# Expert weights loaded in the attention tail, two down projections per row half, and a new order of shared and routed pairs in a mixture-of-experts decoder block

## The chip, the cores and the metric

The kernel runs on one core of one Trainium2 chip. Its time is the device time of one launch in microseconds (us). TensorE is written PE, VectorE DVE, ScalarE ACT, GpSimd POOL and SyncE SP, as in the profile; SP computes nothing and issues most of the DMAs.

## The reference

One decoder layer in fp32 on 4096 tokens (64 sequences of 64) of width 256. Two attention blocks come first, then a mixture of experts: each token has 8 of 64 small experts, and a shared one that all tokens use.

```
x = LN(x + self_attention(x));  x = LN(x + cross_attention(x, ctx))
topv, topi = top_k(x @ gate_w.T, 8);  rw = softmax(topv)
for a routed expert e of a token:  (silu(x @ gate_e.T) * (x @ up_e.T)) @ down_e.T * rw_e     # 64 inner columns
shared: sigmoid(x @ g1.T) * ((silu(x @ sh_gate.T) * (x @ sh_up.T)) @ sh_down.T)
x = LN(x + sum of the 8 routed + shared)
```

## The kernel before

Three phases follow each other, with a clearing of semaphores and a barrier of all engines between them.

**Attention phase.** 32 tiles of 128 tokens go through a software pipeline of six stages, a to f; a step of the pipeline works on six tiles at once, each in another stage. POOL scatters the finished rows of a tile, once per chosen expert, into `slot_scratch`, a DRAM table with a region per expert (`scatter`, L484, 8 indirect DMAs a tile). The rows also go to `token_row_scratch` and the routing data to `route_scratch`, by SP (L322, L328). At the end POOL waits until its scatters have landed.

**Expert phase.** A step works on a pair of row tiles, 2 x 128 rows. The 16 shared pairs (`SHARED_STEPS`) take rows of `token_row_scratch` in order, and only then come 160 sparse pairs (`SPARSE_STEPS`, 320 routed tiles) from `slot_scratch`. Which rows and which expert a routed tile has is found out on the chip: DVE makes tables (`table_counts` to `table_starts`, spread over steps 0 to 6), SP writes them to DRAM and reads them back (`pass_tables`) and takes each tile's address from them (`load_sparse`). For a step s the engines do:

- SP: load of the rows into `x_in[s % 8]`, 8 steps ahead (L1274 for shared pairs, two issues at L1298 for sparse ones)
- PE, in iteration i: `turn_x(i)` (4 transposes, L1377), `gate_and_up(i-1)` (4 matmuls, L1396), `turn_inner(i-2)` (2 transposes, L1405), `project(i-3)` (2 down projections of 64 rows by 256 columns, both on `dp[0:64]`, L1417)
- ACT: copies of the transposes and the silu
- DVE: gate times up, the copy of the result out of `bank_y` into `y[s % 4]` (`copy_y`, L1616, L1620), and three small operations for the destination rows
- POOL: two indirect DMAs of 128 rows per sparse pair to `expert_out_scratch` (`scatter`, L1347); a shared pair is stored by SP (L1260)

`copy_y(s)` waits until `y[s % 4]` has left. The weights of the experts (`gu` 8.4 MB, `dp` 4.2 MB) are loaded in this phase by SP, a group of three pairs of experts per shared step (`load_group`). From sparse pair 8 on, DVE also extracts the routing weights, one operation of 128 x 512 per step, 96 in all (`find_weights`).

**Combine phase.** 32 tiles: the 9 rows of a token are read back, weighted, summed and normalised.

## Time and profile before

| | |
|---|---|
| three timed runs | 1800.71, 1806.1 and 1807.99 us; median 1806.1 |
| profiled execution | 1804.36 us, its span 1802.4 us |
| attention phase, until POOL begins the expert phase | 0 to 1094.5 us |
| expert phase until POOL's first scatter | 1094.5 to 1200.5 us |
| expert phase, POOL's 320 scatters | 1200.5 to 1640.4 us |
| combine phase | 1651.3 us to the end |

A row of a timeline has the start, the duration, the engine, the line, the operation, what it writes and reads, and how many are merged; in brackets is the idle time of the engine before it and what ended it. "issue" is time in which nothing that the profile shows was waited for. PE matmuls are pipelined and their modelled ends overlap, so a stage's length is read from one start to the next. PE's records count two for an fp32 matmul and one for a transpose.

### The profile page before, as it was taken

To read this page: it belongs to the slowest core of one execution; us is meant where nothing else is said; L and a number is where in the kernel's file an instruction comes from. 1 tells how busy PE (TensorE), PEld (TensorE's weight loads), DVE (VectorE), ACT (ScalarE), POOL (GpSimd) and SP (SyncE) were. 2 spreads that over 40 slices of the span, in tenths; PEclk is the share of its full clock that TensorE was granted. 3 is DMA by queue.
4 is the path that set the end of the run, shared out by engine and by line. 5 is a ranking of instruction groups with operands and counts; after the bars stand their busy time and mean duration, and the time that the engine had idled before them with its cause. 6 is when DMAs were issued, how large, how long until landed. Compare 5 with 4: busy or idle time off the path is not lost. (4 is left out here: it accounts for less than half of the span.)

```text
span 1802.4 us, 34145 instructions
## 1 busy us (share of the span) xinstructions
PE 1475.3 (82%) x9600; PEld 1233.7 (68%) x9600; DVE 1319.6 (73%) x3879; ACT 694.7 (39%) x1462; POOL 1109.3 (62%) x1090
## 2 busy tenths in 40 slices
PE   3679999999999899999999855779999999992000
PEld 2568888888888787888888744567777777771000
DVE  3458888888888888888888843147777765553898
ACT  3235444545453444444443412124444444441221
POOL 3328676767676667677776641027777777774444
PEclk8789999999999999999999977579999999996555
DMA  5861212121212112121212117976655556642886
GB/s 197 287 201 50 84 49 77 54 79 51 76 56 74 56 63 69 53 79 47 85 47 71 45 70 230 256 214 191 188 187 185 184 182 189 190 120 99 294 298 241
DMA packets 161421, 237.36 MB, mean 132 GB/s; under 512 B 28044, under 2 KB 135578, under 8 KB 156836
## 3 DMA queue, kind: packets, MB, share of 16 engines
q1 hardware_dynamic: 127636, 160.73, 29.2%
q0 software_dynamic: 27648, 69.28, 10.4%
q10 hardware_dynamic: 6032, 6.13, 1.0%
q8 instruction: 45, 0.74, 0.2%
q14 instruction: 60, 0.49, 0.1%
HBM read 127.47 MB, written 116.93 MB: 136 GB/s over the span
## 5 line engine op out<-in xcount | busy, mean ns | idle before, releaser
L1347 POOL DMA_INDIRECT expert_out_scratch<-y,target x320 | 319.1, 997 | 225.5 <-issue 107.4
L484 POOL DMA_INDIRECT slot_scratch<-xrow x256 | 272.2, 1063 | 187.8 <-DVE xrow L1100 111.6
L1438 ACT ACTIVATE x_turned<-bank_x 128x512 f32<-128x512 f32 x176 | 105.1, 597 | 281.1 <-PE bank_x L1377 281.0
L523 PE MATMUL bank_c<-wq_w,x1t 128*128 128x512 f32 x768 | 193.2, 403 | 15.4 <-DVE q_work L942 11.7
L1417 PE MATMUL bank_y<-dp,inter_t 64*128 (+1 forms) x704 | 205.7, 414 | 0.0
L1396 PE MATMUL bank_g<-gu,x_turned 128*128 (+1 forms) x1408 | 195.6, 284 | 0.0
L669 PE MATMUL bank_d<-wo_w,o2t 128*128 128x256 f32 x1536 | 193.4, 286 | 2.0 <-DVE o2t L858 2.0
L669 PEld LDWEIGHTS bank_d<-wo_w,o2t 128*128 128x128 f32 x1536 | 187.6, 192 | 3.1 <-DVE o2t L858 2.7
L1616 DVE COPY y<-bank_y 128x512 f32<-128x512 f32 x160 | 110.6, 691 | 97.1 <-PE bank_y L1417 97.1
L429 POOL TENSOR_TENSOR q_rs<-q_ve,minus_half 128x8 f32<-128x8 f32 x64 | 137.4, 2147 | 71.3 <-DVE q_ve L933 67.6
L523 PEld LDWEIGHTS bank_c<-wq_w,x1t 128*128 128x128 f32 x768 | 142.3, 190 | 56.6 <-DVE q_work L942 21.0
L1396 PEld LDWEIGHTS bank_g<-gu,x_turned 128*128 128x128 f32 x1408 | 180.4, 200 | 0.7 <-issue 0.7
L1377 PE MATMUL bank_x<-identity,x_rows 128*128 128x128 f32 x704 | 120.8, 296 | 48.6 <-DMA x_rows<-token_row_scratch 39.5
L1417 PEld LDWEIGHTS bank_y<-dp,inter_t 64*128 64x128 f32 x704 | 121.8, 192 | 47.7 <-issue 36.4
L1377 PEld LDWEIGHTS bank_x<-identity,x_rows 128*128 128x128 f32 x704 | 77.5, 146 | 109.1 <-issue 76.6
L742 ACT ACTIVATE q_work<-q_work 128x512 f32<-128x512 f32 x128 | 80.6, 630 | 170.6 <-DVE q_work L942 169.6
L634 PEld LDWEIGHTS bank_c<-k2t,stage_b 128*128 128x128 f32 x1024 | 116.7, 192 | 11.3 <-issue 11.3
L1607 DVE TENSOR_TENSOR inter<-silu,bank_g 128x128 f32<-128x128 f32 x176 | 50.6, 288 | 99.8 <-ACT silu L1445 87.5
L634 PE MATMUL bank_c<-k2t,stage_b 128*128 128x64 f32 x1024 | 121.1, 276 | 0.8 <-ACT stage_b L731 0.8
L942 DVE TENSOR_TENSOR q_work<-bank_c,bq_b 128x512 f32<-128x512 f32 x128 | 86.4, 687 | 21.8 <-PE bank_c L523 21.2
L523 PE MATMUL bank_c<-wkv_w,ctxt 128*128 128x512 f32 x384 | 97.5, 402 | 0.0
L1771 DVE SCALAR_TENSOR_TENSOR total<-rows,w,total 128x256 f32<-128x256 f32 x160 | 92.2, 576 | 1.3
(232 smaller groups left out, 3074.0 us busy)
## 6 DMA issues: line engine op xcount, KB each, us to landing
x_rows<-slot_scratch SPq DMA_DIRECT2D x320, 136.0 KB
rows<-expert_out_scratch SPq DMA_DIRECT2D x32, 1152.0 KB, 5.6
slot_scratch<-zeros SPq DMA_DIRECT2D x18, 1088.0 KB, 11.8
gu<-in_gate_up SPq DMA_DIRECT2D x11, 768.0 KB, 12.5
expert_out_scratch<-y,target POOLq DMA_INDIRECT x320
token_row_scratch<-xrow SPq DMA_DIRECT2D x32, 136.0 KB, 1.8
x_rows<-token_row_scratch SPq DMA_DIRECT2D x16, 272.0 KB
dp<-in_down SPq DMA_DIRECT2D x22, 192.0 KB, 13.7
```

Of the source, the lines that this page charges most:

```text
L429: nc.gpsimd.tensor_tensor(out_, base, minus_half[:, 0:width], ALU.pow).then_inc(sig[done], 1)
L484: nc.gpsimd.indirect_dma_start(out=slot_d[:, :], out_offset=bass.IndirectOffsetOnAxis(ap=xrow[slot][:, SLOT8 + k:SLOT8 + k + 1].bitcast(U3 ...
L523: last = nc.tensor.matmul(target, left[a][:, c, :], right(b, c), start=(n == 0 and c == 0), stop=(n == len(PASSES) - 1 and c == C - 1))
L634: last = nc.tensor.matmul(bank_c[:, n, p * S:(p + 1) * S], q2t[:, n, 2 * p:2 * p + 2, :].rearrange("p h s -> p (h s)"), k2t[:, p // 2, n * ...
L669: last = nc.tensor.matmul(bank_d[:, 0, 0:D], o2t[a][:, h, :], wo_w[b][:, h, :], start=(n == 0 and h == 0), stop=(n == len(PASSES) - 1 and ...
L1347: nc.gpsimd.indirect_dma_start(out=y_d[:, :], out_offset=bass.IndirectOffsetOnAxis(ap=target[s % 8][:, j:j + 1], axis=0), in_=y[s % 4][:, ...
L1377: mm = nc.tensor.transpose(bank_x[:, s % 2, (2 * j + c) * P:(2 * j + c + 1) * P], x_in[s % 8][:, j, c * P:(c + 1) * P], identity[:, :])
L1396: mm = nc.tensor.matmul(bank_g[:, s % 2, j * P:(j + 1) * P], xt[s % 2][:, j, c, :], w, start=(c == 0), stop=(c == C - 1))
L1417: mm = nc.tensor.matmul(bank_y[:, s % 2, j * D:(j + 1) * D], inter_t[s % 2][:, j * P:(j + 1) * P], dp_flat[:, bass.ds(first, D)], start=Tr ...
L1438: nc.scalar.activation(xt[s % 2][:, :, :, :].rearrange("p j c n -> p (j c n)"), bank_x[:, s % 2, :], ACT.Copy).then_inc(sig["x_copied"], 1)
L1616: nc.vector.tensor_copy(y[s % 4][:, :, :].rearrange("p j d -> p (j d)"), bank_y[:, s % 2, :])\
L1771: nc.vector.scalar_tensor_tensor(total[t % 4][:, :], rows[t % LOADS][:, k, :], w8[:, t, k:k + 1], (total if k else joined)[t % 4][:, :], A ...
```

## The change

- The expert weights are loaded by SP in the attention phase: `load_gate_up` once the last tile's projections are done, `load_down` once its cross-attention output is. `gu` and `dp` lie over buffers of the attention phase that are then dead. POOL no longer waits for its row scatters; SP does before the first sparse load.
- `dp` has all 65 experts on partitions 0 to 63, and on partitions 64 to 127 a ring of 8 single experts and the shared one. Each sparse pair loads the down weights of its second tile into the ring (a third DMA in `load_sparse`), when `project(s-8)` is done.
- One transpose of 128 x 128 turns both tiles' inner values, and the two down projections read partitions 0 to 63 and 64 to 127, into two banks. `bank_y` is one pair of banks, not two: `project(s)` waits for `copy_y(s-1)`.
- Six shared pairs run first, then sparse pairs, with one shared pair after every 16th sparse one, ten in all.
- The tables are made in DVE's steps 0, 1 and 2, with seven small operations more; SP passes them before its load of step 6.

```diff
+GU_W = EPAIRS * 512 + 256
+DP_W = 2 * EPAIRS * D
+SHARED_FIRST = 6
...
+            def load_gate_up():
+                sp.wait_ge(sig["qk_projected"], TILES)
...
+                sp.wait_ge(sig["v2_projected"], TILES)
+                groups = gu[:, 0:EPAIRS * 512].rearrange("p (g n) -> p g n", g=GROUPS)
+                for g in range(GROUPS):
+                    sp.dma_start(groups[:, g, :], gate_up[g, :, :]).then_inc(weights["gu_in"], 16)
+
+            def load_down():
+                sp.wait_ge(sig["q_transposed"], 2 * TILES)
+                sp.wait_ge(sig["cross_proj"], TILES)
+                own = dp[0:INNER, :].rearrange("p (g a h n) -> p g a h n", g=GROUPS, a=GROUP, h=2)
+                for g in range(GROUPS):
+                    for h in range(2):
+                        sp.dma_start(own[:, g, :, h, :],
+                                     down[g, h * INNER:(h + 1) * INNER, :].rearrange("p (a n) -> p a n", a=GROUP))\
+                          .then_inc(weights["dp_in"], 16)
...
+                if c is not None and isinstance(c.n, int) and c.n == TILES - 1:
+                    load_gate_up()
+                if e is not None and isinstance(e.n, int) and e.n == TILES - 1:
+                    load_down()
                 at_slot(e, store_row)
                 at(e, store_meta)
...
-            for slot in range(2):
-                pool.wait_ge(sig[f"scattered{slot}"], 16 * TOP_K * (TILES // 2))
...
+        later = SHARED_STEPS - SHARED_FIRST
+        order = [("shared", k) for k in range(SHARED_FIRST)]
+        for n in range(SPARSE_STEPS):
+            order.append(("sparse", n))
+            if later and n % 16 == 15 and n // 16 < later:
+                order.append(("shared", SHARED_FIRST + n // 16))
...
                 if s >= 8:
                     sp.wait_ge(sig["x_turned"], s - 7)
+                    if sparse(s):
+                        sp.wait_ge(sig["y_ready"], s - 7)
...
+                at = sp.snap(regs[3], min_val=0, max_val=(GROUPS * P - INNER) * GROUP + GROUP - 1)
+                sp.dma_start(dp[INNER:P, s % 8 * D:(s % 8 + 1) * D], down_rows[bass.ds(at, INNER, GROUP), :])\
+                  .then_inc(done, 16)
+
+            def load(s):
+                if not sparse(s):
+                    load_shared(s)
+                    return
+                if number(s) == 0:
                     pass_tables()
                     sp.wait_ge(sig["tables_in"], 48)
+                    for slot in range(2):
+                        sp.wait_ge(scattered[slot], 16 * TOP_K * (TILES // 2))
                 load_sparse(s)
+
+            for s in range(8):
+                load(s)
+            for s in range(STEPS):
+                if not sparse(s):
+                    store_shared(s)
+                if s + 8 < STEPS:
+                    load(s + 8)
+                if s == 1:
+                    sp.dma_start(metas[:, :, :], meta_d.rearrange("(t p) e -> p t e", p=P))\
+                      .then_inc(sig["metas_in"], 16)
+                    sp.dma_start(slots[:, :, :], row_d[:, SLOT8:SLOT8 + TOP_K].bitcast(U32)
+                                 .rearrange("(t p) k -> p t k", p=P)).then_inc(sig["slots_in"], 16)
...
-                for j in range(2):
-                    mm = nc.tensor.transpose(bank_i[0:INNER, s % 2, j * P:(j + 1) * P], inter[s % 2][:, j, :],
-                                             identity[:, :])
-                mm.then_inc(sig["inner_turned"], 1)
...
+                nc.tensor.transpose(bank_i[:, s % 2, 0:P], inter[s % 2][:, :, :].rearrange("p j x -> p (j x)"),
+                                    identity[:, :]).then_inc(sig["inner_turned"], 1)
 
             def project(s):
+                if s == 0:
+                    pe.wait_ge(weights["dp_in"], 16 * (2 * GROUPS + 1))
                 pe.wait_ge(sig["inner_copied"], s + 1)
-                if s >= 2:
-                    pe.wait_ge(sig["y_copied"], s - 1)
...
+                if s >= 1:
+                    pe.wait_ge(sig["y_copied"], s)
+                own = held[s][1] if sparse(s) else shared_at[1]
+                ring = s % 8 if sparse(s) else 8
+                nc.tensor.matmul(bank_y[:, 0, 0:D], inter_t[s % 2][0:INNER, :], dp[0:INNER, bass.ds(own, D)],
+                                 start=True, stop=True)
+                nc.tensor.matmul(bank_y[:, 1, 0:D], inter_t[s % 2][INNER:P, :], dp[INNER:P, ring * D:(ring + 1) * D],
+                                 start=True, stop=True).then_inc(sig["y_ready"], 1)
...
+            tables = {0: [table_counts, table_whole, table_tiles] + [lambda k=k: table_scan(k) for k in range(6)],
+                      1: [table_opened] + [lambda c=c: table_find(c) for c in range(3)],
+                      2: [table_depth, table_rows, table_starts]}
```

SP's order at the end of the attention phase and the beginning of the expert phase, before (`UNCONDITIONAL_BRANCH` is where one phase ends and the next begins, `x_scratch` holds the output of the first attention block):

```order
L322 DMA token_row_scratch<-xrow 128x272
L328 DMA route_scratch<-meta 128x128
L125 UNCONDITIONAL_BRANCH
L1247 UNCONDITIONAL_BRANCH
L1274 DMA x_rows<-token_row_scratch 128x2x272
L1252 DMA gu<-in_gate_up 128x1536
L1254 DMA dp<-in_down 64x768 x2
L1274 DMA x_rows<-token_row_scratch 128x2x272 x7
L1305 DMA metas<-route_scratch 128x32x128
L1306 DMA slots<-token_row_scratch 128x32x8
L1252 DMA gu<-in_gate_up 128x1536
L1254 DMA dp<-in_down 64x768 x2
```

The same engine after the change, from the 11 loads of `gu` to the barrier:

```order
L345 DMA gu<-in_gate_up 128x1536 x11
L329 DMA token_row_scratch<-xrow 128x272
L335 DMA route_scratch<-meta 128x128
L317 DMA x_res<-x_scratch 128x256
L329 DMA token_row_scratch<-xrow 128x272
L335 DMA route_scratch<-meta 128x128
L353 DMA dp<-in_down 64x3x256 x22
L356 DMA dp<-in_down 64x256
L329 DMA token_row_scratch<-xrow 128x272
L335 DMA route_scratch<-meta 128x128
L134 UNCONDITIONAL_BRANCH
L1294 UNCONDITIONAL_BRANCH
```

All weight loads stand ahead of the barrier now, and the stores of the last tile's rows and routing data stand behind the 23 loads of `dp`. SP's order in the expert phase after the change, from the six shared loads to the first sparse pair's loads:

```order
L1317 DMA x_rows<-token_row_scratch 128x2x272 x6
L1323 DMA first_scratch<-rowi 128x6
L1324 DMA bound_scratch<-bounds 128x3x3
L1326 DMA place_scratch<-place 128x6
L1328 DMA rows<-first_scratch 1x768
L1329 DMA places<-place_scratch 1x768
L1330 DMA slot_of<-bound_scratch 128x3x320
L1339 TENSOR_LOAD rows
L1342 ISA
L1343 DMA x_rows<-slot_scratch 128x272
L1342 ISA
L1343 DMA x_rows<-slot_scratch 128x272
```

A little further on, behind the loads of steps 8 and 9, SP has the two large loads and then the store of the third shared pair (L1300):

```order
L1345 DMA dp<-in_down 64x256
L1367 DMA metas<-route_scratch 128x32x128
L1369 DMA slots<-token_row_scratch 128x32x8
L1300 DMA expert_out_scratch<-y 128x2x256
L1339 TENSOR_LOAD rows
```

The tables stand ahead of every shared store, and `metas` and `slots` ahead of the third one. On PE, in the middle of the sparse pairs, one pair's last two stages and the next `turn_x` were, before:

```order
L1405 MATMUL bank_i<-identity,inter 64x128 x2
L1417 ISA
L1417 MATMUL bank_y<-dp,inter_t 128x256
L1417 ISA
L1417 MATMUL bank_y<-dp,inter_t 128x256
L1377 MATMUL bank_x<-identity,x_rows 128x128 x4
```

and are after the change:

```order
L1455 MATMUL bank_i<-identity,inter 128x128
L1466 ISA
L1466 MATMUL bank_y<-dp,inter_t 128x256
L1468 MATMUL bank_y<-dp,inter_t 128x256
L1429 MATMUL bank_x<-identity,x_rows 128x128 x4
```

One transpose and one register operation are gone; the two projections stand back to back.

## Rows read from the trace of the kernel before

**Rows 1.** Windows: us, busy PE, PEld, DVE, ACT, POOL, PEclk, DMA share, GB/s

```profile
1094.50:1200.40 105.90, 76.67 (x350) 59.59 (x350) 32.16 (x160) 25.46 (x59) 1.10 (x8) 0.65 0.90 251
1200.40:1640.40 440.00, 433.18 (x2820) 340.35 (x2818) 281.05 (x1345) 186.46 (x470) 319.06 (x320) 0.99 0.56 175
```

**Rows 2.** Timeline of PE over one sparse pair

```profile
1214.32 1.13 PE L1417 MATMUL bank_y<-dp,inter_t 64*128 x4
1215.38 0.66 PE L1377 MATMUL bank_x<-identity,x_rows 128*128 128x128 f32 x4
1215.88 1.06 PE L1396 MATMUL bank_g<-gu,x_turned 128*128 x8
1216.77 0.38 PE L1405 MATMUL bank_i<-identity,inter 128*64 128x128 f32 x2
1217.08 1.13 PE L1417 MATMUL bank_y<-dp,inter_t 64*128 x4
```

**Rows 3.** Timeline of POOL, in mid phase and at the end of the sparse pairs

```profile
1216.95 0.97 POOL L1347 DMA_INDIRECT expert_out_scratch<-y,target  x1 [0.51 <-issue]
1218.23 0.97 POOL L1347 DMA_INDIRECT expert_out_scratch<-y,target  x1 [0.30 <-issue]
...
1633.03 0.97 POOL L1347 DMA_INDIRECT expert_out_scratch<-y,target  x1 [0.30 <-issue]
```

**Rows 4.** SP: its waits from 1300 to 1500 (us, times, longest), and two issues

```profile
SPq L1268 <- DVE named L1589: 76.2, 72, 1.2
...
1187.39 0.85 SPq L1298 DMA_DIRECT2D x_rows<-slot_scratch  x2
```

**Rows 5.** Timeline, waits, landing times and a DVE window of the phase's start

```profile
1094.54 0.20 POOL L1326 MEMSET identity<- 128x128 f32 x1 [6.05 <-POOLq L72]
...
1095.90:1118.50 22.60, 12.27 (x87) 0.76 1.05 304
...
1102.43 7.46 SPq L1306 DMA_DIRECT2D slots<-token_row_scratch  x1
...
1157.00 2.62 SPq L1280 DMA_DIRECT2D first_scratch<-rowi  x1
...
1179.50 1.11 PE L1377 MATMUL bank_x<-identity,x_rows 128*128 128x128 f32 x4 [7.96 <-DMA x_rows<-slot_scratch]
...
1200.46 1.00 POOL L1347 DMA_INDIRECT expert_out_scratch<-y,target  x1 [104.60 <-DVE target L1599]
...
token_row_scratch<-xrow SPq DMA_DIRECT2D x32, 136.0 KB, 1.8
...
slots<-token_row_scratch SPq DMA_DIRECT2D x1, 128.0 KB, 12.2
```

**Rows 6.** Timeline of PE and SP at the end of the attention phase

```profile
1020.38 3.05 PE L523 MATMUL bank_c<-wkv_w,ctxt 128*128 128x512 f32 x12
1060.51 8.33 PE L669 MATMUL bank_d<-wo_w,o2t 128*128 128x256 f32 x48 [2.02 <-DVE o2t L858]
...
1077.71 0.33 SPq L322 DMA_DIRECT2D token_row_scratch<-xrow  x1
```

**Rows 7.** Timeline of PE in the attention phase, cross-attention's matmuls of 64 rows

```profile
716.93 1.14 PE L658 MATMUL bank_d<-stage_b,v 64*128 64x256 f32 x8
717.99 0.71 PE L565 MATMUL bank_b<-p1t,v 128*128 128x128 f32 x4
```

**Rows 8.** Timeline of PE over one pair at the lower clock

```profile
1188.77 0.63 PE L1405 MATMUL bank_i<-identity,inter 128*64 128x128 f32 x2
1189.34 2.07 PE L1417 MATMUL bank_y<-dp,inter_t 64*128 64x256 f32 x4
...
1193.95 0.63 PE L1405 MATMUL bank_i<-identity,inter 128*64 128x128 f32 x2
```

**Rows 9.** Windows of the scatters alone: us, busy POOL, PEclk, DMA share, GB/s

```profile
1350.00:1470.00 120.00, 91.20 (x88) 1.00 0.58 183
1213.00:1350.00 137.00, 96.70 (x100) 1.00 0.61 191
```

More of the change, by code:

```diff
@@ L66, in decoder @@
     w8 = kept.enter_context(nc.sbuf_tensor("w8", [P, TILES, TOP_K], F32))
+    weights = {name: kept.enter_context(nc.semaphore(name)) for name in ("gu_in", "dp_in")}
+    scattered = [kept.enter_context(nc.semaphore(f"scattered{n}")) for n in range(2)]
+    xrow = [kept.enter_context(nc.sbuf_tensor(f"xrow{n}", [P, XW], F32)) for n in range(2)]
+    with ExitStack() as place:
+        gu = place.enter_context(nc.sbuf_tensor("gu", [P, GU_W], F32))
+        dp = place.enter_context(nc.sbuf_tensor("dp", [P, DP_W], F32))
     attention = {name: nc.alloc_semaphore(name) for name in ATTENTION_SIGNALS}
     attention_phase(nc, attention, x, ctx, mask, qkv, o_proj, gamma, beta, wq, bq, wk, bk, wv, bv, wo, qn_w, kn_w,
-                    router, x1_d, slot_d, row_d, meta_d, count, jump)
+                    router, x1_d, slot_d, row_d, meta_d, count, jump, gate_up, down, gu, dp, weights,
+                    scattered, xrow)
     nc.clear_and_free_semaphores(list(attention.values()))
@@ L73, in decoder @@
     expert = {name: nc.alloc_semaphore(name) for name in EXPERT_SIGNALS}
-    expert_phase(nc, expert, gate_up, down, slot_d, row_d, meta_d, y_d, place_d, first_d, bound_d, count,
-                 jump, w8)
+    expert_phase(nc, expert, slot_d, row_d, meta_d, y_d, place_d, first_d, bound_d, count, jump, w8, gu, dp,
+                 weights, scattered, down)
     nc.clear_and_free_semaphores(list(expert.values()))
@@ L210, in attention_phase @@
         h2_rs = sb("h2_rs", [P, 1])
-        xrow = [sb(f"xrow{n}", [P, XW]) for n in range(2)]
         zeros = sb("zeros", [P, XW])
@@ L1160, with expert_phase @@
 """.split()
-def expert_phase(nc, sig, gate_up, down, slot_d, row_d, meta_d, y_d, place_d, first_d, bound_d, count, jump, w8):
+def expert_phase(nc, sig, slot_d, row_d, meta_d, y_d, place_d, first_d, bound_d, count, jump, w8, gu, dp, weights,
+                 scattered, down):
     with ExitStack() as stack:
@@ L1175, in expert_phase @@
         inter = [sb(f"inter{n}", [P, 2, INNER]) for n in range(2)]
-        inter_t = [sb(f"inter_t{n}", [INNER, 2 * P]) for n in range(2)]
+        inter_t = [sb(f"inter_t{n}", [P, P]) for n in range(2)]
         y = [sb(f"y{n}", [P, 2, D]) for n in range(4)]
@@ L1189, in expert_phase @@
         pair = sb("pair", [P, 3])
+        group = sb("group", [P, 3])
+        by_pair = sb("by_pair", [P, 3])
+        by_group = sb("by_group", [P, 3])
         earlier = sb("earlier", [P, 3])
@@ L1288, in pass_tables @@
                   .then_inc(sig["tables_in"], 16)
-            regs = [sp.alloc_register(f"row_reg{n}") for n in range(2)]
+            regs = [sp.alloc_register(f"row_reg{n}") for n in range(4)]
+            down_rows = down.rearrange("g p (a n) -> (g p a) n", a=GROUP)
             def load_sparse(s):
                 free_rows(s)
-                i = 2 * (s - SHARED_STEPS)
-                sp.reg_load(regs, rows[0:1, i:i + 2])
+                i = 2 * 2 * number(s)
+                sp.reg_load(regs, rows[0:1, i:i + 4])
+                done = sig[f"x_in{s % 8}"]
@@ L1306, in _ @@
[L1306 to L1314 removed]
+                    at = sp.snap(regs[2 * j], min_val=1, max_val=SLOT_ROWS - P)
@@ L1321, in _ @@
             for n in range(4):
-                sp.wait_ge(sig[f"y_stored{n}"], 16 * (SHARED_STEPS // 4))
+                sp.wait_ge(sig[f"y_stored{n}"], 16 * sum(not sparse(s) for s in range(n, STEPS, 4)))
         @block.gpsimd
@@ L1331, in _, with fill @@
                 nc.gpsimd.memset(scan[n][:, 0:EXPERTS], 0.0).then_inc(sig["cleared"], 1)
-            def number(out, pattern, base, step):
+            def fill(out, pattern, base, step):
                 nc.gpsimd.iota(out, pattern, base=base, channel_multiplier=step,
                                allow_small_or_imprecise_dtypes=True).then_inc(sig["numbered"], 1)
-            number(base[:, :], [[REGION, EXPERTS]], 1, 0)
-            number(which[:, :], [[1, 3]], 0, 3)
-            number(part[:, :], [[0, 1]], 0, 1)
-            number(column[:, :], [[1, TOP_K]], 0, 0)
+            fill(base[:, :], [[REGION, EXPERTS]], 1, 0)
+            fill(which[:, :], [[1, 3]], 0, 3)
+            fill(part[:, :], [[0, 1]], 0, 1)
+            fill(column[:, :], [[1, TOP_K]], 0, 0)
             def scatter(s):
-                n = s - SHARED_STEPS
+                n = number(s)
                 pool.wait_ge(sig["y_copied"], s + 1)
@@ L1392, in gate_and_up @@
                 for j in range(2):
-                    first = held[s][j][0] if sparse(s) else shared_at[0]
+                    first = held[s][2 * j] if sparse(s) else shared_at[0]
                     for c in range(C):
@@ L1652, in _ @@
                     stage()
-                if s == SHARED_STEPS:
+                now = s < STEPS and sparse(s)
+                if now and number(s) == 0:
                     table_slots()
-                if sparse(s) and s < STEPS:
+                if now:
                     match_row(s)
@@ L1658, in _ @@
                     gate_inner(s - 1)
-                if sparse(s) and s < STEPS:
+                if now:
                     name_row(s)
@@ L1662, in _ @@
                     copy_y(s - 3)
-                if sparse(s) and s < STEPS:
+                if now:
                     bound_row(s)
-                n = s - SHARED_STEPS - 8
+                n = number(s) - 8 if now else None
                 if n == -1:
@@ L1668, in _ @@
                     nc.vector.tensor_copy(slots_f[:, :, :], slots[:, :, :]).then_inc(sig["slots_as_float"], 1)
-                elif 0 <= n < 3 * TILES:
+                elif now and 0 <= n < 3 * TILES:
                     find_weights(n)
```

189 lines of the change are left out of this document (87 added, 102 removed).

## Prediction

> **What bounds the kernel now.** I read the windows by stage first. The scatter stretch is 440 us long and PE is busy for 433 of them at almost the full granted clock, 2.4 GHz; ahead of it stand 106 us of start-up in which DMA is busy to 90% and the clock is 0.65 on average [rows 1]. Then the timeline of one sparse pair: from one `project` to the next, 1214.32 to 1217.08, it is 2.76 us, and PE's four groups fill it without a gap. Read from start to start, `project` takes 1.06, `turn_x` 0.50, `gate_and_up` 0.89 and `turn_inner` 0.31 us [rows 2]. 160 pairs by 2.76 are 441 us: PE sets this stretch. The next engine is close. POOL's two scatters of a pair begin at 1216.95 and 1218.23, 0.97 us each, idle 0.51 us ahead of the first and 0.30 ahead of the second; near the end, where PE has finished, a pair's first scatter too comes 0.30 behind the one before [rows 3]. So POOL can't do a pair in less than 2 x (0.97 + 0.30), with rounding 2.55 us, and has only 0.2 us of slack. SP waits 76.2 us in 72 pairs, 1.06 us of 2.76, so its own use is 1.70 [rows 4].
>
> In the start-up POOL begins at 1094.54, after 6.05 us of idle, so its last scatter of rows ended at 1088.5; the tables are sent at 1157.0, the first sparse transpose is at 1179.5 and the first scatter at 1200.46 [rows 5]. Nearly all of these 106 us are 16 shared pairs fed by queues full of weights.
>
> **The sum, term by term.** I count to the end of POOL's scatters, 1640.4; the combine phase is unchanged.
>
> *The attention tail.* `gu` is issued after the last projection, which begins at 1020.38 and lasts some 3 us [rows 6]. 8.4 MB at the 251 GB/s of the start-up window [rows 1] are 33 us, done by about 1057. `dp` comes after the output product, 1060.51 plus 8.3: 23 loads. An issue costs about 0.43 us (two in 0.85 us [rows 4]), so 10 us, to 1079; its 4.2 MB take 17 us at that rate, to 1086. The last row store moves from 1077.7 to about 1080 and lands with `dp` at 1087, just under POOL's 1088.5 [rows 5, 6]. Price nothing if so; if `dp` holds the stores up, up to 10 us. POOL's dropped wait for its landings is worth 1 us (a landing is 1.8 [rows 5], most of it hidden by the clearing). The barrier then ends at 1093.5: gain 1, bounds -10 and +2.
>
> *Start of the expert phase.* DVE was busy 12.3 us between 1095.9 and 1118.5, and that holds all tables, six gate products and six halves of shared results [rows 5]. Bunched, with seven small operations more, I take 11.5 us; they start 1.4 us after the phase, so they are ready at 1106.5. Sending and reading back are two round trips: six issues (3 us) and two landings of 2 to 3 us; the first sparse load lands 3 us later. PE then has its first sparse rows at about 1117, where it had them at 1179.5. Six shared pairs don't fill that time.
>
> What is late next is SP. Behind the loads of steps 8 and 9 stand `metas` and `slots`; the issue of `slots` held SP for 7.46 us and landed after 12.2 [rows 5]. The store of the third shared pair is behind them, and `copy_y(6)`, the first sparse result, waits for that store, since it is in the same `y` buffer; the rows of step 10 are behind it too. SP reaches `metas` at 1121, leaves `slots` at 1129, and the store lands behind the data of both, at 1136. First scatter at 1137.5, where it was 1200.5: gain 63 (the 1 us of the tail in it). Bounds: 1129 if the store isn't held up, 1150 if it is and the loads behind it as well.
>
> *The pace of the sparse pairs.* `turn_inner` loses one transpose of the kind of which `turn_x` does four in 0.50: 0.12 us [rows 2]. For `project` the trace has a near case in cross-attention: there four matmuls of 64 rows (8 records) alternate between the two halves of the partitions and take 716.93 to 717.99, 1.06 us [rows 7], as long as two matmuls (4 records) on one half in the expert phase [rows 2]. So I take it that two on different halves run together. At the lower clock `project`'s group lasts 2.07, at the higher 1.13 us [rows 2, 8]: 0.94 of it scales, some 0.12 is fixed, and two together need 0.12 + 0.47 = 0.6 us. Gain 0.46, bounds 0 (they don't overlap) and 0.53 (exactly half). PE: 2.76 - 0.12 - 0.46 = 2.2 us. DVE's 281 and ACT's 186 us of work [rows 1] are 1.76 and 1.17 in a pair, stay as they are and fit. SP adds one issue with its register work: 0.43 at least, 0.85 (half of what a pair's two take now) at most, I take 0.5, which makes 2.2. POOL is unchanged at 2.55 and so becomes the bound. The new wait for `copy_y` costs nothing: the copy begins when `project` ends, and `turn_x`, `gate_and_up` and `turn_inner` of the next iteration, 0.50 + 0.89 + 0.2 = 1.6 us, stand between it and the next `project`; without that cover the whole copy would be PE's wait.
>
> Scatters are not always 0.97. From 1213 to 1350 100 of them take 96.7 us, from 1350 to 1470 88 take 91.2 us, 1.036 each, 0.07 more [rows 9], and `find_weights` works in both. I take half of that for the 96 pairs with `find_weights`: 96 x 2 x 0.035 = 7, with rounding 8 us; bounds 0 and, if all 96 go at the old 2.76, 20. The Trainium skill, SBUF — State Buffer, § Who interferes with whom, has DVE operations with two SBUF inputs contend with a GpSimd instruction that reads SBUF, and lets those with one input alone. By it the products of `find_weights` could hold a scatter and its reduction could not; the rows show delays in one stretch and none in the other, so the trace bears it out at most in part.
>
> PE may start at 1.2 GHz: there a pair took 1188.77 to 1193.95, 5.2 us, with 2.07 for `project` and 0.57 for `turn_inner` [rows 8]. `project` falls to half, 1.04, and `turn_inner` to some 0.4: 4.0 us. Four such pairs cost 4 x 1.45 = 6 us.
>
> The ten late shared pairs have no scatter. 17 pairs on PE are 37.4 us, 16 on POOL 40.8: hidden behind POOL. Without that cover (POOL not the bound) they cost 2.2 each, 22 us.
>
> The stretch is 160 x 2.55 + 8 + 6 = 422 us, where it was 440: gain 18.
>
> Sum: 63 + 18 = 81 us. POOL ends at about 1559.5 instead of 1640.4, the profiled execution takes 1804.4 - 81 = 1723. The median of the runs shown is 1.7 us above the profiled execution, so I say **1725 us**, 4.5% less.
>
> **The rivals.**
>
> *POOL at the old pace* (chance 0.17). Its slack of 0.2 us is used up by collisions with DVE, as between 1350 and 1470. For: POOL now sets DVE's moments, so that it may lock into the bad phase. Against: the 100 scatters before that took 0.967 each [rows 9]. All pairs at 2.76: 441 + 6 = 447, 25 more than the sum: 1750.
>
> *The projections don't overlap* (0.05). PE at 2.76 - 0.12 = 2.64 with 170 pairs, 449 + 6, 33 more: 1758. For: no row has two projections on two halves. Against: rows of cross-attention [rows 7].
>
> *A start-up held by DMA* (0.14). `dp` delays the last stores and `slots` the first sparse pairs, both at their bounds: 11 + 12.5, 1748. For: DMA was at 90% there [rows 1]. Against: 12.6 MB of it are gone from this stretch.
>
> *Slower: PE falls to 1.2 GHz* (0.06). PE was busy without a gap and is to wait 0.35 us in every pair; the clock is 0.65 in the start-up, where PE waits for rows, and 0.99 in the stretch without gaps [rows 1]. At the lower level a pair costs 4.0 us, 1.45 over POOL's. The gain of 81 is used up when 81/1.45 = 56 of 170 pairs run so; with half of them, 85, it is 123 us more: 1848. Against: once there, PE is busy without a gap and would rise again. The Trainium skill, TensorE: Matmul & The Clock Gate, § A second HAM failure mode: psum-queue depth-cycling, describes a clock that swings between its two levels when PE idles briefly between groups of matmuls. By it this rival is the likelier outcome; no row of this loop has such gaps.
>
> *Faster still* (0.08): no hold-up at `slots`, no half clock, no collisions: 1137.5 becomes 1129 and 14 us go from the stretch: 1702.
>
> The likeliest case has 0.50. Its own range is 1710 to 1742. For 8 in 10 I take in the faster case and the first three rivals: 1702 to 1758. Runs of this kernel differ by 0.4%, so I count 0.5% as no change. Faster by more: 0.93, all cases but the slower one and a part of it; within: 0.02, a clock that is low for a third of the pairs; slower: 0.05.
>
> **What would show it.** The first scatter at 1137 (the step of the start-up); gaps between scatters of 0.30 throughout (POOL the bound); from `project` to the next `turn_x` 0.6 us; PE waiting some 0.35 us per pair, at a granted clock of 1.0; no change of pace at each seventeenth pair; SP still waiting a little in each pair. Wrong would be a pace above 2.76 us per pair, a granted clock of 0.5 in the stretch, a DMA share near 1 there (0.56 x 440/422 and, by 64 KB more beside four tiles of 128 to 136 KB, an eighth more: 0.66), or a barrier after 1100.

## The result and the profile after

The changed kernel takes 1736.03 us (median of 4, 1735.02 to 1736.81), the kernel before 1807.05 us beside it: ratio 0.960, 95% interval 0.9572 to 0.9627. The forecast was 1725 us, in a range of 1702 to 1758. The profiled execution took 1735.31 us, its span is 1733.3 us.

| us from the span's start | before [rows 1, 5] | forecast | after |
|---|---|---|---|
| POOL begins the expert phase | 1094.5 | 1093.5 | 1103.7 |
| tables sent | 1157.0 | 1106.5 | 1116.1 |
| first sparse transpose | 1179.5 | 1117 | 1129.6 |
| first scatter | 1200.5 | 1137.5 | 1149.8 |
| end of POOL's scatters | 1640.4 | 1559.5 | 1570.3 |
| first scatter to that end | 440 | 422 | 420.5 |

The pace came as forecast, and from the phase's start to the first scatter it is within 2 us of it (46.1 for 44); the attention tail ended 10 us later than forecast.

The page's group of the scatters, and the window of the scatter stretch (columns as in [rows 1]):

```profile
L1397 POOL DMA_INDIRECT expert_out_scratch<-y,target x320 | 317.8, 993 | 147.5 <-issue 83.9
...
1149.70:1567.00 417.30, 390.70 (x2844) 293.05 (x2844) 290.25 (x1379) 173.85 (x501) 315.09 (x318) 0.98 0.74 225
```

320 scatters now take 318 us of 420, and the 319 gaps of 0.30 us between them another 96: POOL is free for 7 us of the stretch, 4.1 of them behind the first pair. PE is at 0.98 of its full clock, and the DMA share is 0.74, where 0.66 was forecast.

One sparse pair on PE, timeline, to be laid beside [rows 2]:

```profile
1250.64 0.27 PE L1455 MATMUL bank_i<-identity,inter 128*128 128x128 f32 x1
1250.84 0.48 PE L1466 MATMUL bank_y<-dp,inter_t 64*128 x1
1250.85 0.48 PE L1468 MATMUL bank_y<-dp,inter_t 64*128 64x256 f32 x1
...
1251.16 0.38 PE L1466 MATMUL bank_y<-dp,inter_t 64*128 x1
1251.17 0.38 PE L1468 MATMUL bank_y<-dp,inter_t 64*128 64x256 f32 x1
...
1251.48 0.66 PE L1429 MATMUL bank_x<-identity,x_rows 128*128 128x128 f32 x4
...
1252.86 0.27 PE L1455 MATMUL bank_i<-identity,inter 128*128 128x128 f32 x1
```

The two projections start 0.01 us apart, twice; `project` takes 0.64 us to the next `turn_x` (forecast 0.6), and from one `turn_inner` to the next it is 2.22 us (forecast 2.2). A little later the same page shows what PE now waits for, all engines in one stretch:

```profile
1431.29 0.97 POOL L1397 DMA_INDIRECT expert_out_scratch<-y,target  x1 [0.31 <-issue]
...
1431.44 0.69 DVE L1676 COPY y<-bank_y 128x512 f32<-128x512 f32 x1 [1.71 <-DMA expert_out_scratch<-y,target]
...
1432.37 0.48 PE L1466 MATMUL bank_y<-dp,inter_t 64*128 x1 [0.93 <-DVE y L1676]
...
1432.57 0.97 POOL L1397 DMA_INDIRECT expert_out_scratch<-y,target  x1 [0.30 <-issue]
```

The chain is that of a pace set by POOL: its scatters stand 1.28 us apart, `copy_y` waits for the landing of an earlier scatter, `project` waits for `copy_y`. At times PE catches up with this limit and then waits for up to 1.9 us at once. Between 1200 and 1500, some 117 pairs, SP still waits 14.0 us for `project` in 21 waits, and 29 us in all: it has slack, but not in each pair, as was forecast.

The end of the attention tail and the start of the expert phase, on SP and POOL, and SP's wait at the barrier:

```profile
1075.88 14.72 SPq L353 DMA_DIRECT2D dp<-in_down  x22
...
1091.52 0.37 SPq L329 DMA_DIRECT2D token_row_scratch<-xrow  x1
...
SPq L409 <- DMA token_row_scratch<-xrow: 8.5, 1, 8.5
...
1094.38 0.97 POOL L517 DMA_INDIRECT slot_scratch<-xrow  x1 [0.30 <-issue]
1103.71 0.20 POOL L1376 MEMSET identity<- 128x128 f32 x1 [8.35 <-POOLq L80]
...
1136.52 5.46 SPq L1369 DMA_DIRECT2D slots<-token_row_scratch  x1
1142.02 4.23 SPq L1300 DMA_DIRECT2D expert_out_scratch<-y  x1
...
1149.79 0.99 POOL L1397 DMA_INDIRECT expert_out_scratch<-y,target  x1 [44.76 <-DVE target L1659]
```

Two things are new. POOL's last scatter of rows ends at 1095.35, 6.9 us later than before, and from there to the next phase it is 8.35 us, not 6.05. The second is SP's: its last store stands behind the data of `dp` and lands 9 us after its issue. The first begins some 60 us earlier, on PE. The score products of tile 31, with a 5 us window around their start (columns as in [rows 1]), of the kernel before and then of the changed one:

```profile
1035.56 3.79 PE L634 MATMUL bank_c<-k2t,stage_b 128*128 128x64 f32 x32
...
1035.00:1040.00 5.00, 5.00 (x45) 4.67 (x42) 3.45 (x11) 1.08 (x2) 1.27 (x1) 0.98 0.02 3
```

```profile
1037.19 7.09 PE L665 MATMUL bank_c<-k2t,stage_b 128*128 128x64 f32 x32
...
1035.00:1040.00 5.00, 5.00 (x24) 4.09 (x23) 2.00 (x7) 2.11 (x3) 1.28 (x1) 0.50 1.03 430
```

PE has the same work and is busy throughout in both. Before, it is granted the full clock; after, half of it, and at the same time the 8.4 MB of `gu` pass at over 400 GB/s. The score products take 3.3 us longer and the output product behind them 2.2 us (8.16 for 5.92).

Of the experiments below, six (`slots` on POOL, `slots` on ACT, `gu` behind everything, the small memset, the pieces of 3 KB, four pairs first) ran while the kernel before, beside them, took 2018 or 2047 us (medians) instead of 1807, with all engines held up again and again for a reason that the traces don't show (the scatter stretch is 588 to 602 us long in them, and POOL doesn't set its pace), so their totals are compared only with those beside them, and their traces read where nothing is held up.

### The profile page after: what moved, and what is told of

It reads as the page before. It is cut to its first block and busy times, and to the rows that moved or that the text cites. A ratio compares the mean times of both kernels' runs of the same rounds, so it can differ in the third digit from the quotient of the medians.

```text
span 1733.3 us, 34126 instructions
## 1 busy us (share of the span) xinstructions
PE 1387.4 (80%) x9424; PEld 1153.3 (67%) x9424; DVE 1318.3 (76%) x3888; ACT 667.8 (39%) x1462; POOL 1109.3 (64%) x1090
## 5 line engine op out<-in xcount | busy, mean ns | idle before, releaser
L700 PE MATMUL bank_d<-wo_w,o2t 128*128 128x256 f32 x1536 | 197.5, 290 | 2.0 <-DVE o2t L889 2.0
L700 PEld LDWEIGHTS bank_d<-wo_w,o2t 128*128 128x128 f32 x1536 | 191.8, 197 | 3.1 <-DVE o2t L889 2.7
L1447 PEld LDWEIGHTS bank_g<-gu,x_turned 128*128 128x128 f32 x1408 | 174.2, 195 | 19.4 <-issue 18.3
L1466 PE MATMUL bank_y<-dp,inter_t 64*128 (+1 forms) x352 | 124.4, 434 | 14.4 <-DVE y L1676 12.5
L1468 PE MATMUL bank_y<-dp,inter_t 64*128 64x256 f32 x352 | 124.6, 434 | 0.0
L647 PE MATMUL bank_c<-identity,q_work 128*128 128x128 f32 x512 | 72.5, 287 | 25.6 <-DVE q_work L983 23.6
## 6 DMA issues: line engine op xcount, KB each, us to landing
slot_scratch<-zeros SPq DMA_DIRECT2D x18, 1088.0 KB, 11.8
```

Source lines behind the costliest of these rows:

```text
L700: last = nc.tensor.matmul(bank_d[:, 0, 0:D], o2t[a][:, h, :], wo_w[b][:, h, :], start=(n == 0 and h == 0), stop=(n == len(PASSES) - 1 and ...
L1447: mm = nc.tensor.matmul(bank_g[:, s % 2, j * P:(j + 1) * P], xt[s % 2][:, j, c, :], w, start=(c == 0), stop=(c == C - 1))
L1466: nc.tensor.matmul(bank_y[:, 0, 0:D], inter_t[s % 2][0:INNER, :], dp[0:INNER, bass.ds(own, D)], start=True, stop=True)
L1468: nc.tensor.matmul(bank_y[:, 1, 0:D], inter_t[s % 2][INNER:P, :], dp[INNER:P, ring * D:(ring + 1) * D], start=True, stop=True).then_inc(si ...
```

## The experiments

Twelve kernels ran.

**Both projections on one half.** The second tile takes the first one's inner values and weights.

```diff
-                nc.tensor.matmul(bank_y[:, 1, 0:D], inter_t[s % 2][INNER:P, :], dp[INNER:P, ring * D:(ring + 1) * D],
+                nc.tensor.matmul(bank_y[:, 1, 0:D], inter_t[s % 2][0:INNER, :], dp[0:INNER, bass.ds(own, D)],
```

> The changed kernel, but both down projections of a pair read partitions 0 to 63 (the second tile takes the inner values and weights of the first, so its result is the first one's); all transfers, copies and scatters stay. Theory A, the projections overlap because they stand on two row halves: from one `project` to the next `turn_x` goes from 0.63 back to 1.06 us, a pair on PE from 2.22 to 2.65, above POOL's 2.555, so that PE sets the pace and the ten late shared pairs are paid too: 160 x 2.555 becomes 170 x 2.65, some 30 to 40 us more, about 1770 us. Theory B, the two matmuls overlap because nothing stands between them and they write two banks: no change, 1735 us.

Measured 1767.8 us (1766.76 to 1769.29). A pair of it on PE, and a window:

```profile
1286.28 0.66 PE L1429 MATMUL bank_x<-identity,x_rows 128*128 128x128 f32 x4
1286.77 1.06 PE L1447 MATMUL bank_g<-gu,x_turned 128*128 x8
1287.67 0.27 PE L1455 MATMUL bank_i<-identity,inter 128*128 128x128 f32 x1
1287.87 0.70 PE L1466 MATMUL bank_y<-dp,inter_t 64*128 x2
1288.40 0.59 PE L1468 MATMUL bank_y<-dp,inter_t 64*128 x2
1288.93 0.66 PE L1429 MATMUL bank_x<-identity,x_rows 128*128 128x128 f32 x4
...
1290.00:1450.00 160.00, 160.00 (x1029) 126.38 (x1028) 116.81 (x524) 63.21 (x183) 111.67 (x115) 1.00 0.71 216
```

The second projection now starts 0.53 us behind the first, a pair takes 2.65 us, PE is busy without a gap, and POOL pauses a whole pair more at each late shared pair (2.7 us, at 1197.5, 1242.5, 1287.5). Theory A, within 3 us of its 1770: two banks alone don't let the projections overlap, the two row halves do, and without the overlap the change gains 41 us instead of 71. Two halves on one bank were not run, so whether the second bank is needed as well stays open.

**All shared pairs first.** `SHARED_FIRST = 16`.

> The changed kernel with all 16 shared pairs ahead of the sparse ones, as before the change. Theory A, POOL sets the pace and the late shared pairs are hidden behind it: the stretch of the scatters stays at 420 us (160 x 2.555 and some), and the first scatter comes later by ten shared pairs less the time in which PE waited for the first sparse rows: 10 x 2.2 to 2.6 less 8, that is 14 to 18 us, about 1751 us. Theory B, PE sets the pace: the stretch gets 22 us shorter by what the start gets longer, within 5 us of 1735.

Measured 1753.91 us (1750.84 to 1754.79). The first scatter is at 1170.1 and the last ends at 1588.3: 418 us, where the changed kernel has 420.5. The order gives nothing to the pace; it moves the first scatter, to 67.5 us after the phase's start instead of 46.1. The ten late pairs cost the stretch 2.5 us together, where ten pairs on PE would be 22: they are nearly free. Theory A.

**`metas` and `slots` later, by SP.** `if s == 1` becomes `if s == 6`.

> The changed kernel, but the two large loads `metas` and `slots` are issued behind the store of the sixth shared pair and the rows of step 14, instead of ahead of the third one's store. Theory A, the first sparse result waited for that store: it lands 6 to 10 us earlier, the first scatter moves from 46 us after the phase's start to 37 or 40, and the end moves with it: 1727 to 1730 us. Theory B, the first sparse pair is bound by its rows and the tables, and the store only comes last by chance: the first scatter moves by less than 2 us, 1734 to 1735 us. A third possibility, the hold-up only moves on to the rows of steps 15 and 16: scatters start early but pause later, within 3 us of 1735.

Measured 1737.08 us (1728.75 to 1738.83). The third possibility. The first scatter comes 39.3 us after the phase's start, so theory A was right on what held it up; but SP's 5.5 us for `slots` and the data before it now stand ahead of the rows of step 15 (timelines of SP, PE and POOL):

```profile
1151.55 5.48 SPq L1369 DMA_DIRECT2D slots<-token_row_scratch  x1
1158.02 4.67 SPq L1343 DMA_DIRECT2D x_rows<-slot_scratch  x2
...
1165.25 1.11 PE L1429 MATMUL bank_x<-identity,x_rows 128*128 128x128 f32 x4 [9.49 <-DMA dp<-in_down]
...
1165.86 0.97 POOL L1397 DMA_INDIRECT expert_out_scratch<-y,target  x1 [9.40 <-DVE y L1676]
```

The 7 us won at the first scatter are lost in two pauses, of 9.4 us ahead of the eleventh scatter and of 2.8 us ahead of the thirteenth.

**`dp` behind the last rows' stores.** `load_down()` is called behind `store_meta`.

> The changed kernel, but the 23 loads of `dp` are issued behind the stores of the last tile's rows and routing data, not ahead of them. The stores then land after 2 us, not after 9. Theory A, the barrier waited 2.3 us beyond POOL's last scatter for those stores only: SP, issuing 0.64 us each from 1086, is done at 1100.5, so the barrier is within 2 us of where it is now (1103.7), and `dp` lands some 10 us later, which the six shared pairs feel: the first result comes later, but the first scatter within 3 us. 1733 to 1740 us. Theory B, `dp`'s data hold up the whole phase's start: its rows and tables wait for them, and the end comes 5 to 10 us later, 1740 to 1745 us.

Measured 1738.84 us (1729.26 to 1743.3). SP issues the 23 loads from 1085.42 to 1100.5, the phase begins at 1104.1 and the first scatter is at 1153.4, 49.3 us behind. Removing the wait for the stores gains nothing, since SP's own issuing takes its place: theory A on the barrier, and some of theory B behind it (the first scatter is 3.2 us further from the phase's start than in the changed kernel). The total lies in theory A's range.

**`gu` behind everything.** `load_gate_up()` is called behind the last tile's `store_meta`.

> The changed kernel, but the 11 loads of `gu` are issued behind the last tile's stores (and so behind `dp`), not in the middle of the attention tail. Theory A, PE's clock stays at 1.2 GHz between 1030 and 1046 because of the 33 us of weight traffic that begin at 1025: without it the score products of the last tile are back at 3.8 us (7.1 in the changed kernel) and POOL's last scatter of rows ends at about 1089 to 1090, not 1095. Theory B, the clock is low for a reason of its own (the tail's work comes some 1.2 us later than before): the score products still take about 7 us and the last scatter ends at 1094 to 1096. In both cases SP's 11 further issues put the barrier later and `gu` lands only in the expert phase, where the first shared pair waits for it, so the whole is slower, some 1745 to 1760 us.

Measured 1987.16 us, ratio to before 0.984. The score products of tile 31, and the window around them:

```profile
1110.34 3.76 PE L665 MATMUL bank_c<-k2t,stage_b 128*128 128x64 f32 x32
...
1110.00:1115.00 5.00, 4.96 (x45) 4.69 (x42) 3.77 (x11) 1.29 (x3) 1.56 (x2) 1.00 0.07 25
```

3.76 us at the full clock, as before the change; the three kernels beside it that kept `gu` in its place have 7.09 each. The price of the move was forecast rightly in kind: the first scatter is 59.2 us behind the phase's start, and the total 7 us above that of the kernel with the small memset beside it. By itself this is theory A, and so it was taken for the runs that followed; three of them contradict it (below).

**`slots` by POOL, and by ACT.**

```diff
-                if s == 1:
-                    sp.dma_start(metas[:, :, :], ...
-                    sp.dma_start(slots[:, :, :], ...
+            nc.gpsimd.dma_start(metas[:, :, :], ...
+            nc.gpsimd.dma_start(slots[:, :, :], ...
```

> The changed kernel, but `metas` and `slots` are loaded by POOL at the start of the expert phase, where it has nothing to do for 45 us, instead of by SP. Theory A, what came late at the first scatter was SP behind these two: the first scatter comes 37 to 40 us after the phase's start (46 in the changed kernel), with no pause of 9 us behind it as in the run with `slots` moved back, so 7 to 9 us are gained: 1726 to 1729 us. Theory B, the 4096 short rows of `slots` cost the same time on the DMA engines wherever they are issued, and now they stand before the first rows of the phase: tables and shared pairs start later, 1735 us or more.

> The same with ACT issuing the two loads ahead of its first copy. Theory A: ACT is held some 6 us, so the first shared pair and with it the second and third part of the tables come 3 to 4 us later; SP is free as with POOL. First scatter 40 to 43 us after the phase's start, 1729 to 1732 us. Theory B as for the run with POOL: 1735 us or more.

Measured 1971.79 us with POOL, ratio 0.978, and 1970.96 us with ACT, ratio 0.975. From the phase's start to the first scatter it is 40.2 us with POOL and 42.3 with ACT; the kernel with the small memset beside them, in which SP loads `slots`, has 46.4. Theory A, in both, by the first scatter; the totals are 9 us below that kernel's, but in these runs POOL doesn't set the pace.

**A memset more per pair on POOL.** `nc.gpsimd.memset(spare[:, 2 * n:2 * n + 2], 0.0)` ahead of a pair's scatters, and then one of 448 columns.

> The changed kernel with one memset of 128 x 2 more on POOL per sparse pair, ahead of its two scatters. Theory A, POOL sets the pace of the scatters: each of the 160 memsets is paid in full, by its own time and the gap that it adds, 0.1 to 0.25 us each, 16 to 40 us in all: 1751 to 1775 us. Theory B, SP's three loads or PE's 2.22 us set it and POOL only looks busy: less than 5 us, up to 1740.

Measured 1980.45 us, ratio 0.980, and no test of anything: POOL's timeline shows the memset inside the 0.30 us between two scatters (next scatter 0.32 us after the last one's end). The wide one doesn't fit there:

> The changed kernel with one memset of 128 x 448 more on POOL per sparse pair, ahead of its two scatters. In the run before, a memset of 128 x 2 between two scatters that stand back to back took 0.13 us and fell into the 0.30 us that lie between them anyway, so that it said nothing; memsets of 128 x 128 and 128 x 272 take 0.20 and 0.32 us in the trace of the changed kernel, so this one takes some 0.48. Theory A, POOL sets the pace: each adds 0.3 to 0.55 us to a pair of 2.555, 48 to 88 us in all, 1784 to 1824 us. Theory B, SP's three loads or PE's 2.22 us set it: POOL's own slack takes it, under 10 us, up to 1746.

Measured 1786.86 us (1783.06 to 1787.86), 51 us more than the changed kernel:

```profile
1254.74 0.97 POOL L1400 DMA_INDIRECT expert_out_scratch<-y,target  x1 [0.31 <-issue]
1255.70 0.50 POOL L1398 MEMSET spare<- 128x448 f32 x1
1256.37 0.97 POOL L1400 DMA_INDIRECT expert_out_scratch<-y,target  x1 [0.17 <-POOL spare L1398]
```

The scatters stand 0.66 us apart where the memset is, 0.36 more than 0.30: 160 x 0.36 = 58 us, and the stretch is 475.6 us, 55 more. POOL sets the pace. The total of this execution rose by 48 us only because its attention tail was 6.6 us shorter: `gu` stands where the changed kernel has it, and yet the score products of tile 31 and the window around them are

```profile
1035.90 3.79 PE L665 MATMUL bank_c<-k2t,stage_b 128*128 128x64 f32 x32
...
1035.00:1040.00 5.00, 5.00 (x44) 4.58 (x41) 3.10 (x11) 1.36 (x3) 1.27 (x1) 0.95 1.01 422
```

that is, 422 GB/s of traffic and a clock of 0.95.

**`gu` a step later and `slots` on POOL.** `load_gate_up()` is called behind `store_meta` of the step in which it stood ahead of `store_row`.

> Two edits to the changed kernel: `gu` is issued behind the row and routing stores of the step in which it now stands ahead of them (by some 16 us later, when the last tile's score products are done), and POOL instead of SP loads `metas` and `slots` at the start of the expert phase. Theory A, the clock is held low by the weight traffic only where both meet: the score products take 3.8 us instead of 7.1, POOL's last scatter of rows ends 3 to 6 us earlier (output product of the same tile unchanged or slower), and the first scatter comes 38 to 41 us after the phase's start, not 46: together 8 to 13 us, 1723 to 1728 us. Theory B, the low clock only moves with the traffic to the work behind it (the output product, at 1.2 GHz 8 us instead of 6, and the last tile's products): 1727 to 1731 us, and if moving `slots` doesn't help either, 1735.

Measured 1725.65 us (1719.19 to 1728.11), ratio to the kernel before 0.9532, 95% interval 0.9508 to 0.9557; the changed kernel has 0.960. It is the fastest of the versions that ran beside a kernel before of 1807 to 1809 us, by some 10 us; the two built on it below ran beside one of 2047 us and can't be compared with it. The profiled execution is the fastest of the six.

```profile
1034.84 3.76 PE L665 MATMUL bank_c<-k2t,stage_b 128*128 128x64 f32 x32
1038.41 5.99 PE L700 MATMUL bank_d<-wo_w,o2t 128*128 128x256 f32 x48
...
1087.63 0.97 POOL L517 DMA_INDIRECT slot_scratch<-xrow  x1 [0.30 <-issue]
1096.19 0.20 POOL L1371 MEMSET identity<- 128x128 f32 x1 [7.59 <-POOLq L80]
...
1099.36 1.73 POOL L1389 DMA_DIRECT2D slots<-token_row_scratch  x1
1136.86 1.05 POOL L1397 DMA_INDIRECT expert_out_scratch<-y,target  x1 [35.77 <-DVE target L1659]
```

In this execution both products are at their old durations, POOL's last scatter of rows ends at 1088.6 as before the change, and the first scatter comes 40.7 us behind the phase's start, without a long pause after it. The second is what `slots` on POOL gives; that the first is due to the place of `gu` doesn't hold, as the next two show. The other five executions, without a trace, took 1724 to 1728 us.

**`dp` in pieces of 3 KB.**

```diff
-                        sp.dma_start(own[:, g, :, h, :],
-                                     down[g, h * INNER:(h + 1) * INNER, :].rearrange("p (a n) -> p a n", a=GROUP))\
+                        at = (h * EPAIRS + g * GROUP) * D
+                        sp.dma_start(dp[0:INNER, at:at + GROUP * D], down[g, h * INNER:(h + 1) * INNER, :])\
```

> The run with `gu` later and `slots` on POOL, and besides the experts of `dp` laid out in two halves, so that a load of `dp` in the attention tail writes 3 KB in one piece per partition, as before the change, and not three of 1 KB. Theory A, the small pieces make the loads slow: an issue takes 0.43 us again instead of 0.65, the 22 loads hold SP 10 us instead of 15, their data move at 300 GB/s and more instead of 210, the last stores (9 us behind them) land 4 us sooner, and the barrier is 2 to 4 us earlier, then limited by POOL's last scatter: 1722 to 1724 us where that run had 1725.7. Theory B, the pieces make no difference in time: 1725 to 1726.

Measured 1995.51 us, ratio 0.974. The 22 issues take 14.20 us (0.65 each; 0.67 and 0.68 with small pieces in the changed kernel and the run before), and from POOL's last scatter to the phase it is 7.59 us, as in the run before. In 15 us over their issues 220 GB/s pass, and 223 in the changed kernel. Theory B: the pieces make next to no difference. In it `gu` is issued at 1131.8, and the score products of tile 31, with no transfer beside them, are

```profile
1127.21 7.09 PE L664 MATMUL bank_c<-k2t,stage_b 128*128 128x64 f32 x32
...
1125.00:1130.00 5.00, 5.00 (x24) 4.09 (x23) 1.98 (x7) 2.11 (x3) 1.28 (x1) 0.50 0.01 3
```

**Four shared pairs first.** `SHARED_FIRST = 4`, one shared pair behind each 13th sparse pair.

> The same with four shared pairs ahead of the sparse ones and twelve behind each 13th sparse pair. Theory A, from the first sparse load to the first scatter (17 us in the run with `slots` on POOL) SP is the limit: behind the first sparse load it issues the rows of three more steps and a shared pair's store between each, 2.75 us a step; with two shared pairs fewer ahead, four sparse loads follow each other at 1.6 us, and the first scatter comes 3 to 5 us earlier, while the twelve late shared pairs stay hidden behind POOL: 1718 to 1721 us. Theory B, PE at 1.2 GHz and the round trip of the tables are the limit, or the extra late pairs show: within 2 us of the run before it.

Measured 2004.77 us, ratio 0.980; the run with 3 KB pieces, beside it and otherwise the same, had 1995.51. SP's loads do come closer together, 2.1 us a step, but the first scatter is 40.0 us behind the phase's start, 0.8 less than with six. Theory B on the first scatter. The median is 9 us higher, outside theory B's 2 us, while the two traced executions took the same (1998.6 and 1998.9), and since POOL doesn't set the pace here, whether twelve late pairs stay hidden was not settled. What lies between the first sparse load and the first scatter isn't SP. Which of PE's slow clock and the round trips it is was not separated.

## Why the prediction was right, and where not

**The pace.** Right in its mechanism. `project` 0.64 us for 0.6, PE's pair 2.22 for 2.2, POOL the bound at 2.555 a pair, the stretch 420.5 us for 422; the runs with one half and with the wide memset show both causes by themselves. The price of a start at the lower clock was 6 us, for four pairs: in the stretch one pair ran so (the window from 1150 to 1155 has a granted clock of 0.52), and the pause behind the first pair of scatters, from PE's wait for its loads until 1150.3 and from this clock together, is 4.4 us. As a mean the clock is 0.98, with PE busy 391 of 417 us, but it did fall once more in the middle of the sparse pairs, behind a wait of PE for `copy_y` (timeline of PE, and a window with the columns of [rows 1]):

```profile
1259.33 0.47 PE L1466 MATMUL bank_y<-dp,inter_t 64*128 x1 [1.70 <-DVE y L1676]
...
1260.80 2.07 PE L1447 MATMUL bank_g<-gu,x_turned 128*128 x8 [0.18 <-issue]
...
1260.00:1265.00 5.00, 4.82 (x27) 3.65 (x26) 3.03 (x16) 1.25 (x4) 3.78 (x5) 0.66 0.51 170
```

`gate_and_up` takes 2.07 us there and not 1.06, and the clock is back after some 3.4 us; POOL's scatters stand 0.30 apart throughout, so nothing of it reaches the time. The run with `gu` later and `slots` on POOL has two such falls in its stretch, the one with all shared pairs first has four, and the kernel before, where PE is busy for 433 of 440 us, has none while the pairs last. The Trainium skill, TensorE: Matmul & The Clock Gate, § A second HAM failure mode: psum-queue depth-cycling, by which the clock could swing, is borne out in kind and not in weight: one fall behind the start in 417 us. By the rival's own price it takes 56 slow pairs to use up the gain.

**The collisions.** Forecast 8 us, measured 6.5 (22 scatters of 1.05 to 1.49 us instead of 0.97). The forecast took them from a mean; the single rows say more, from the timeline of POOL and DVE:

```profile
1241.08 0.68 DVE L1703 TENSOR_REDUCE w<-w_match 128x8 f32<-128x512 f32 x1
1241.12 0.97 POOL L1397 DMA_INDIRECT expert_out_scratch<-y,target  x1 [0.31 <-issue]
...
1250.05 0.68 DVE L1693 TENSOR_TENSOR w_match<-metas,slots_f 128x512 f32<-128x512 f32 x1
1250.25 1.33 POOL L1397 DMA_INDIRECT expert_out_scratch<-y,target  x1 [0.30 <-DVE y L1676]
```

Sorting all 320 scatters of a trace by what DVE does at their start: in the changed kernel 28 begin inside one of the two products of `find_weights` and take 1.20 us on average, 13 inside its reduction and 87 inside `copy_y`, 0.97 us each; before, 27 inside a product (1.16 and 1.37 us), 14 inside the reduction, 0.97. The Trainium skill, SBUF — State Buffer, § Who interferes with whom, says just this of DVE operations with two SBUF inputs against those with at most one, and the traces agree. In these rows a scatter loses what is left of the product less some 0.1 us (0.36 of 0.48 in the row above); two that begin less than 0.03 us behind the start of one lose nothing, and there the product takes 0.72 and 0.74 us for 0.68. So the phase between the two engines decides, and that is why one stretch of before had none: no scatter of before begins inside a product until 1365. The prediction called the skill's rule borne out at most in part; by the single rows it is borne out, and that half of the mean came near is luck.

**The start of the expert phase.** 46.1 us from the phase's start to the first scatter for the 44 of the sum, where it was 106 before; of the 63 us forecast for the first scatter, tail and start together, 50.7 came, and 10 of the 12 missing are the tail's. `slots` and the store behind it held up the first scatter, as said; SP was held 5.46 and 4.23 us there. Moved to POOL the two are worth 5.4 us.

**The attention tail.** This is the step that failed: a gain of 1 us, with 10 us of loss as the bound, and it was 9.2 us of loss. Three parts. (1) PE's clock, 5.5 us: neither the sum nor a rival had the tail's matmuls at another clock than before. The changed kernel's four executions lie within 1.8 us of each other, so its median most likely holds this loss. (2) "An issue costs about 0.43 us": that is the rate of the row loads; the issues of `dp` took 0.67, so 23 took 15.3 us and not 10. The trace of before had rows for the same data (timeline of SP), 0.85 us each in this one and 0.55 to 0.6 in most of the later ones, and they should have been used:

```profile
1095.48 1.70 SPq L1254 DMA_DIRECT2D dp<-in_down  x2
```

 (3) The row store behind `dp` was issued at 1091.5 for 1080 and landed 9.3 us later for 7, at 1100.8: the forecast had it at 1087, just under the end of POOL's scatters, and it came 5.4 us behind that end. Of (2) and (3) together 2.3 us show at the barrier (8.35 us from POOL's last scatter for 6.05); the barrier came after 1100, which the prediction had named as a sign of being wrong. The remaining 1.2 us or so were there before anything was changed in the order (SP's stores at 1005.66 for 1004.43): two executions differ by that much.

The sum: 10.2 us at the phase's start, 2.1 to the first scatter, 1.5 back in the stretch, 1 in the combine phase (163 for 162 us), 11.8 in all, nearly all of the 12 by which the profiled execution is above the 1723 of the sum. The rival "a start-up held by DMA" and the bound of 10 us in the sum had the tail's loss rightly in size and not in its cause: more than half of it was the clock. So the total lies in the range of the likeliest case, 1710 to 1742, with some luck.

## What to carry over

Count to the next engine before crediting a faster one: PE gained 0.54 us a pair, but POOL stood 0.2 us behind it, and the pace moved by that. What a freed engine then buys is other work in its shadow, here ten shared pairs that cost next to nothing once they stood behind a scatter. When loads are moved into an idle-looking stretch, price their issue from a row of the same transfer, and look for small stores behind them that a barrier waits for. And an effect of a few us that a single trace shows, such as a clock, is to be looked up in every other trace of the same code before it is given a cause.

## What was not expected of the hardware

The granted clock in the attention tail comes in two ways in traces of the same code. In all 14 traces it falls to 0.50 some 7 to 9 us ahead of the score products of tile 31, where PE waits for DVE, ACT and POOL. In four it is back at 1.00 when these begin, and they take 3.76 to 3.79 us; in ten it comes back only 9 to 12 us after they begin, though PE is busy without a gap in between, and they take 7.09. With `gu` passing beside them the clock was late in eight traces and in time in one (the wide memset); with `gu` elsewhere it was late in two (the wide rows, four first) and in time in three (before, `gu` behind everything, `gu` a step later). So the traffic is neither needed for the late clock nor brings it about each time. Whether it makes it more frequent, and what decides, stays open. The executions without a trace can't be sorted so, but two of them point to the same: one of four with `slots` later and one of four with `dp` behind the stores took 1729 us at a mean granted clock of 0.913 and 0.912, the other six 1737 to 1743 us at 0.907 to 0.911.
